# A GRU scan on one core: n's columns of W_hh copied by ScalarE as each chunk lands, band loads behind W_hh, and one round of Toeplitz products moved into step 7

## The chip, the cores and the metric

The kernel runs on one core of a Trainium2 chip. The metric is device time in microseconds (us), median of the runs; less is better.

## The reference, cut to what matters

```python
# x: (16, 256, 512) f32, cond: (16, 512); W_ih, W_hh: (512, 1536); b_ih, b_hh: (1536,)
x = x + causal_depthwise_conv(x, cond)   # 16 taps along T=256, one filter value per lag and channel
def cell(h, xt):
    gi = xt @ W_ih + b_ih                # split in three: i_r, i_z, i_n
    gh = h @ W_hh + b_hh                 # h_r, h_z, h_n
    r = sigmoid(i_r + h_r); z = sigmoid(i_z + h_z)
    n = tanh(i_n + r * h_n)
    h_new = (1 - z) * n + z * h
    return h_new, h_new
x = x + scan(cell, h0=cond, over=T)
```

Batch is 16, T is 256, the feature width F is 512, all float32.

## The kernel before

The scan is 256 steps, one after the other, t = 0 to 255. The features lie in C = 4 chunks of 128 partitions; the state and the gates are split in H = 2 halves f, of two chunks each. One step on TensorE is 32 matmuls h @ W_hh (`recur(t, f, c)`, L304, four matmuls of 192 columns each, one for each strip of 32 columns of the array). While VectorE, ScalarE and GpSimd turn the sums into the next h, TensorE fills the time with x @ W_ih for two steps ahead of need (`product(m, f, c)`, L294, four matmuls; a call for each chunk c, four calls a step). Each float32 matmul appears in the trace as two records, so a step's `recur` is 64 records and its products are 32. `pg` are the PSUM accumulators, `hp` the state, `s_h[f]` the semaphore that counts finished states of half f (1 at the start, t + 2 after step t).

**W_hh.** `whh` holds per chunk four blocks of F columns: n, r, z, n. The main loop reads the first three (n, r, z). SyncE loads r, z, n of each chunk into blocks 1 to 3 (L210, 768 KB a chunk, semaphore `s_whh[c]`), and then n of all chunks once more into block 0 (L211, 1024 KB, `s_whn`). Step 0 does not read block 0: `recur_first(f, c)` (L315, L318) takes r, z and the last block in two matmuls, 128 and 64 columns. Between its chunks stand matmuls on zeros, `IDLE` = 4 behind chunk 1 and 3 behind chunk 2 (L373), whose result nobody reads. Before step 1 TensorE waits for `s_whn`.

**The convolution.** Times 0 to 15 are done by VectorE and, for chunk 3, by TensorE. Times 16 to 47 come from TensorE: `turn(p, l, r)` (L332), for each half l of the features 16 rounds r of four matmuls of the band matrix `tz` with a window of x, `xw[l]`, into `pcv`. From time 48 on VectorE does it (L474). The dictionary `ROUNDS` says in which steps the rounds stand: half 0 in steps 6 and 7, half 1 in step 10. VectorE moves the result out of `pcv` (`spread`, steps 8 and 9 and step 11). The first round of a half waits for all eight of its `xw` transfers, and of half 0 also for the eight `tz` transfers.

**SyncE's queue.** After the W_hh transfers SyncE waits for all of them, `s_whn` too, and then goes through the steps: at step t it waits for `s_h[0]` >= t + 1, and issues what stands there: eight band transfers `tz` (L177) at t = 0 to 2 (2, 3 and 3), eight `xw[0]` transfers (L185) at t = 3 to 5 (2, 3, 3), eight `xw[1]` transfers at t = 6 to 8 (2, 3, 3), then later x windows `xb` (L198) and the output. Each `tz` and `xw` transfer is 128 KB in rows of 16 floats.

Of the kernel before, what the change touches and what calls it, by code (L numbers as in the profile page):

```python
# [7 lines left out]
ACT = mybir.ActivationFunctionType  # L8

P = 128  # L10
J, C, D = 4, 4, 32
B, T, F = 16, 256, 512
K = 16
# [16 lines left out]
FEW = 4  # L30
WARM = 6
LATE = 18
IDLE = {1: 4, 2: 3}
M2 = T // 2
RZ, IN, END = CH * D, 3 * CH * D, 4 * CH * D
Q = 3
# [3 lines left out]
def build(nc, x, cond, w_ih, w_hh, b_ih, b_hh, out):  # L40
    assert J * D == P
    ctx = ExitStack()
    with ctx:  # L43
# [20 lines left out]
        whh = sb("whh", [P, C, 4 * F])  # L64
# [82 lines left out]
        def share(total, steps, t):  # L147

            a, b = steps
            return range(total * min(max(t - a, 0), b - a) // (b - a), total * min(max(t + 1 - a, 0), b - a) // (b - a))  # L150


        ROUNDS = {(0, 0): (6, 8), (0, 1): (10, 11)}
        TURNED = {(0, 0): (8, 10), (0, 1): (11, 12)}
        SPANS = [(a - W2 - 4, a - 4) for a, _ in LONG]
        BAND = (0, 3)
# [12 lines left out]
        @block.sync  # L169
        def _(sp):  # L170
            def band(q):
                l, g = divmod(q, G)
                c, e = l * CH + g // 2, g % 2
                if q == 0:
                    sp.wait_ge(s_scr, 16)
                    sp.wait_ge(s_band, 1)
                sp.dma_start(tz[W2 * g:W2 * (g + 1), l, :, g * K:(g + 1) * K],  # L177
                             bass.AP(scratch, (e * C + c) * TAPS, [[1, W2], [2 * C * TAPS, P // 2], [1, K]])
                             ).then_inc(s_tz, 16)

            def load(p, l, q):
                i, g = divmod(q, G)
                t = W2 * p + TB * i
                c, e = l * CH + g // 2, g % 2
                sp.dma_start(xw[l][W2 * g:W2 * (g + 1), :, i, :],  # L185
                             x[:, c, t * B:(t + W2) * B].rearrange("(p e) (w b) -> e w p b", e=2, b=B)[e]
                             ).then_inc(s_xw[p][l], 16)

            def load_long(k, c, i):
                a, b = LONG[k]  # L190
                if i == c == k == 0:
                    sp.wait_ge(s_c3, 1)
                if i == 0 and k >= 2:
                    sp.wait_ge(s_long, len(EVERY) * (k - 2) + K * (c + 1))
                n = (K - 1 + b - a) * B
                at, to = n * i // PIECES, n * (i + 1) // PIECES
                first = (a - K + 1) * B
                sp.dma_start(window(k)[:, c, at:to], x[:, c, first + at:first + to]).then_inc(s_xb[k][c], 16)  # L198

            def store(k, c):  # L200
                a, b = STORES[k]
                sp.wait_ge(s_o, b)
                sp.dma_start(out[:, c, a * B:b * B], x1_of(c, a, b)).then_inc(s_out[k], 16)

            sp.dma_start(cnd[:, :, :], cond).then_inc(s_cnd, 16)  # L205
            sp.dma_start(xs[:, :, :], x[:, :, 0:TB * B]).then_inc(s_xs, 16)  # L206
            for c in range(C):
                sp.dma_start(wih[:, c, :, :], w_ih[:, c, :, :]).then_inc(s_wih[c], 16)  # L208
            for c in range(C):
                sp.dma_start(whh[:, c, F:], w_hh[:, c, :]).then_inc(s_whh[c], 16)  # L210
            sp.dma_start(whh[:, :, 0:F], w_hh[:, :, 2 * F:]).then_inc(s_whn, 16)  # L211
            for c in range(C):
                sp.wait_ge(s_whh[c], 16)
            sp.wait_ge(s_whn, 16)
            for t in range(T):
                sp.wait_ge(s_h[0], t + 1)
                for q in share(2 * G, BAND, t):
                    band(q)
                for (p, l), steps in WINDOWS.items():
                    for q in share(2 * G, steps, t):  # L220
                        load(p, l, q)
                for k in range(len(LONG)):
                    for c in range(C):
                        for i in share(PIECES, arriving(k, c), t):
                            load_long(k, c, i)
                for k, (a, b) in enumerate(STORES[:NB - 1]):
                    for c in share(C, (b, b + C), t):
                        store(k, c)
                for k, (a, b) in enumerate(STORES[NB - 1:-1], NB - 1):
                    if b == t:  # L230
                        sp.wait_ge(s_o, b)
                        sp.dma_start(out[:, :, a * B:b * B], x1_of(slice(None), a, b)).then_inc(s_out[k], 16)
            a, b = STORES[-1]
            sp.wait_ge(s_o, b)
            sp.dma_start(out[:, :, a * B:b * B], x1_of(slice(None), a, b)).then_inc(s_out[len(STORES) - 1], 16)
            for k in range(len(STORES)):
                sp.wait_ge(s_out[k], 16 * (C if k < NB - 1 else 1))
# [40 lines left out]
        def _(pe):  # L278
# [86 lines left out]
                pe.wait_ge(s_h[f], 1)  # L365
            for c in range(C):
                pe.wait_ge(s_whh[c], 16)
                for f in range(H):
                    i = recur_first(f, c)
                    if c == C - 1:  # L370
                        i.then_inc(s_gh[f], 1)
                for _ in range(IDLE.get(c, 0)):
                    pe.matmul(pcv[:, 0:512], zeros[:, 0:P], zeros[:, :], start=True, stop=True)  # L373
            for c in range(C):
                product(2, 0, c)
            pe.wait_ge(s_whn, 16)
            for t in range(1, T):
                m = t // 2
                if t % 2 == 0:
                    pe.wait_ge(s_tin[0], m + 1)  # L380
                    pe.wait_ge(s_tin[1], m + 1)
                pe.wait_ge(s_h[0], t + 1)
                recur(t, 0, 0)
                recur(t, 0, 1)
                recur(t, 1, 0)
                pe.wait_ge(s_h[1], t + 1)
                recur(t, 0, 2)
                recur(t, 0, 3).then_inc(s_gh[0], 1)
                recur(t, 1, 1)
                recur(t, 1, 2)  # L390
                recur(t, 1, 3).then_inc(s_gh[1], 1)
                if m + 2 < M2:
                    for c in range(C):
                        product(m + 2, t % 2, c)
                for (p, l), steps in ROUNDS.items():
                    for r in share(K, steps, t):
                        turn(p, l, r)

        @block.scalar
        def _(act):  # L400
            def seed(m, f):

                if m < Q:
                    act.wait_ge(s_bits, 2 * Q)
                    act.wait_ge(s_bc, H)
                else:
                    act.wait_ge(s_tn[f], 2 * (m - Q) + 2)
                act.activation(pg[m % Q][f][:, 0:END], bc[:, f, :], ACT.Copy).then_inc(s_seed[f], 1)  # L408

            act.dma_start(bih[:, :], b_ih).then_inc(s_small, 16)  # L410
            act.dma_start(bhh[:, :], b_hh).then_inc(s_small, 16)
            act.wait_ge(s_cp, 3)
            act.dma_start(scratch[:, :, :], cpad[:, :, :]).then_inc(s_scr, 16)
            act.wait_ge(s_eye, 2)
            act.wait_ge(s_cnd, 16)
            for lag in range(K):
                act.activation(diagonal(lag), eye[:, :], ACT.Copy, scale=cnd[:, C - 1, K - 1 - lag:K - lag]).then_inc(s_dg, 1)
            for m in range(Q):
                for f in range(H):
                    seed(m, f)  # L420
            act.wait_ge(s_c3, 1)
            act.activation(x1[:, C - 1, 0:TB * B], pcv[:, 0:TB * B], ACT.Copy).then_inc(s_ev, 1)
            act.activation(pre[:, :], cnd[:, 0, :], ACT.Sigmoid)
            act.wait_ge(s_zero, 4)
            for t in range(T):
                u = slice(t % 2 * B, (t % 2 + 1) * B)
                for f in range(H):
                    act.wait_ge(s_trz[f], t + 1)
                    act.activation(rz[:, f, :, :, 1].rearrange("p g (c b) -> p (g c) b", b=B), gt[:, f, :, u],  # L429
                                   ACT.Sigmoid).then_inc(s_rz[f], 1)  # L430
                    act.activation(zcp[:, f, ::2, :, 1], gt[:, f, CH:, u],  # L431
                                   ACT.Sigmoid, scale=-1.0).then_inc(s_zc[f], 1)
                    act.wait_ge(s_an[f], t + 1)
                    act.activation(nzh[:, f, ::2, :, 0], chunks(an[:, f, :, 1]), ACT.Tanh).then_inc(s_n[f], 1)  # L434
                if t % 2 and t // 2 + Q < M2:
                    for f in range(H):
                        seed(t // 2 + Q, f)
# [170 lines left out]
```

## Time and profile before

| | |
|---|---|
| median of 3 runs | 1035.78 us (1035.08 to 1035.82) |
| the profiled execution's own time | 1035.15 us |
| its span in the trace | 1033.4 us |
| mean granted TensorE clock, share of full | 0.996 |
| TensorE matmul busy | 1018.7 us, 99% |
| VectorE busy | 855.9 us, 83% |
| ScalarE busy | 396.8 us, 38% |
| GpSimd busy | 239.1 us, 23% |

Times in the rows are microseconds from the span's start unless marked ns. PE is TensorE, DVE VectorE, ACT ScalarE, POOL GpSimd, SP SyncE; SPq is its queue of issued transfers. The profiled execution took 1.75 us more than its span, for what lies around the span.

### The profile page before, as it was taken

How to read it: one execution, taken by the hardware profiler on the slowest of the kernel's cores; microseconds unless marked ns; L12 is line 12 of the kernel's file. 1: busy time of each engine (PE TensorE's matmuls, PEld its weight loads, DVE VectorE, ACT ScalarE, POOL GpSimd, SP SyncE). 2: the span in 40 equal slices, each digit the busy share in tenths (PEclk: the TensorE clock that was granted, in tenths of full speed). 3: DMA queues.
4: the chain of work that ended last, by engine and by line, in shares of the span. 5: the costliest groups of instructions: out<-in, count | busy, mean ns of one | idle time of the engine just before them, and what ended most of it. 6: DMA issues, size and time to landing. Idle time of an engine off the chain costs nothing.

```text
span 1033.4 us, 58398 instructions
## 1 busy us (share of the span) xinstructions
PE 1018.7 (99%) x24948; PEld 975.6 (94%) x24949; DVE 855.9 (83%) x2838; ACT 396.8 (38%) x1812; POOL 239.1 (23%) x782
## 2 busy tenths in 40 slices
PE   8899999999999999999999999999999999999997
PEld 6779999999999999999999999999999999999996
DVE  7548888888888888888888888888888887777554
ACT  4324334333333343433433433333333343343342
POOL 3212222222222222222222222222222222222222
PEclk9989999999999999999999999999999999999999
DMA  8851000010010101001010010100101000000000
GB/s 312 80 64 34 20 15 31 19 40 19 15 33 14 39 18 29 25 11 36 18 35 24 11 35 15 39 19 20 30 15 35 14 28 16 12 29 3 24 14 12
DMA packets 78930, 33.53 MB, mean 32 GB/s; under 512 B 56016, under 2 KB 77136, under 8 KB 78672
## 3 DMA queue, kind: packets, MB, share of 16 engines
q1 hardware_dynamic: 78240, 29.70, 11.5%
q8 instruction: 196, 3.21, 1.3%
q14 instruction: 62, 0.51, 0.2%
q10 hardware_dynamic: 432, 0.11, 0.0%
HBM read 21.31 MB, written 8.49 MB: 29 GB/s over the span
## 4 chain that ended last, share of the span: by engine, by line
PE 96%; DMA 2%; SPq 1%; DVE 0%; issue 0%; DVEq 0%; POOLq 0%; ACT 0%
PE pg L304 64%; PE pg L294 31%; DMA whh<-w_hh 2%; SPq L185 1%; PE pcv L332 0%; DMA xw<-x 0%; SPq L208 0%; SPq L210 0%; DVE hp L522 0%; DVE gn L501 0%; SPq L206 0%; SPq L205 0%; POOLq L43 0%; DVE an L509 0%; DVEq L520 0%
## 5 line engine op out<-in xcount | busy, mean ns | idle before, releaser
L304 PE MATMUL pg<-whh,hp 128*32 128x192 f32 x16320 | 718.6, 327 | 3.2 <-DVE hp L522 2.5
L304 PEld LDWEIGHTS pg<-whh,hp 128*32 128x32 f32 x16320 | 640.1, 110 | 28.5 <-DVE hp L522 2.3
L294 PE MATMUL pg<-wih,x 128*32 128x192 f32 x8192 | 386.4, 326 | 0.0
L270 POOL TENSOR_TENSOR nzh<-rz,hp 128x32 f32<-128x32 f32 x512 | 157.9, 308 | 788.2 <-ACT rz L429 788.2
L294 PEld LDWEIGHTS pg<-wih,x 128*32 128x32 f32 x8192 | 321.3, 110 | 11.6
L429 ACT ACTIVATE rz<-gt 128x64 f32<-128x64 f32 x512 | 135.9, 266 | 502.8 <-DVE gt L497 477.9
L474 DVE SCALAR_TENSOR_TENSOR x<-xb,cnd,x 128x512 f32<-128x512 f32 (+1 forms) x420 | 294.8, 702 | 7.9
L497 DVE STREAM_TRANSPOSE gt<-pg 128x128 f32<-128x128 f32 x512 | 160.1, 313 | 69.9 <-PE pg L304 61.8
L522 DVE TENSOR_TENSOR_SCAN hp<-zcp,nzh 128x96 f32<-128x96 f32 x512 | 173.3, 338 | 41.6 <-ACT nzh L434 41.0
L509 DVE TENSOR_TENSOR_SCAN an<-rz,gn 128x64 f32<-128x64 f32 x512 | 149.0, 291 | 51.8 <-ACT rz L429 51.6
L434 ACT ACTIVATE nzh<-an 128x32 f32<-128x32 f32 x512 | 120.7, 236 | 126.4 <-DVE an L509 126.4
L431 ACT ACTIVATE zcp<-gt 128x32 f32<-128x32 f32 x512 | 111.0, 217 | 0.0
L501 DVE STREAM_TRANSPOSE gn<-pg 128x64 f32<-128x64 f32 x512 | 107.0, 209 | 0.0
L408 ACT ACTIVATE pg<-bc 128x256 f32<-128x256 f32 x256 | 86.3, 369 | 0.0
L264 POOL TENSOR_TENSOR x<-x,hp 128x64 f32<-128x64 f32 x256 | 82.0, 320 | 0.7 <-DVE hp L522 0.7
L492 DVE STREAM_TRANSPOSE gn<-pg 128x64 f32<-128x64 f32 x256 | 58.0, 227 | 0.0
L474 DVE SCALAR_TENSOR_TENSOR x<-xb,cnd 128x512 f32<-128x512 f32 (+1 forms) x28 | 19.3, 690 | 0.1
L458 DVE SCALAR_TENSOR_TENSOR x<-xs,cnd,x 128x192 f32<-128x192 f32 (+11 forms) x45 | 11.6, 327 | 0.0
L332 PE MATMUL pcv<-tz,xw 128*32 128x64 f32 x256 | 5.0, 243 | 4.4 <-DMA xw<-x 4.4
L332 PEld LDWEIGHTS pcv<-tz,xw 128*32 128x32 f32 x256 | 4.6, 126 | 5.0 <-DMA xw<-x 4.8
L257 POOL MEMSET tz<- 128x8192 f32 x1 | 6.9, 6927 | 1.0 <-DVE bc L543 1.0
L340 PEld LDWEIGHTS pcv<-xs,xb 128*128 128x128 f32 x32 | 4.7, 196 | 0.3
(42 smaller groups left out, 47.1 us busy)
## 6 DMA issues: line engine op xcount, KB each, us to landing
xb<-x SPq DMA_DIRECT2D x96, 94.0 KB, 2.0
out<-x SPq DMA_DIRECT2D x60, 128.0 KB, 1.8
wih<-w_ih SPq DMA_DIRECT2D x4, 768.0 KB, 8.1
whh<-w_hh SPq DMA_DIRECT2D x4, 768.0 KB, 14.5
xw<-x SPq DMA_DIRECT2D x16, 128.0 KB, 4.5
whh<-w_hh SPq DMA_DIRECT2D x1, 1024.0 KB, 18.9
tz<-taps SPq DMA_DIRECT2D x8, 128.0 KB, 4.7
xb<-x SPq DMA_DIRECT2D x16, 62.0 KB, 1.9
```

What stands on the lines that cost most here:

```text
L270: pool.tensor_tensor(nzh[:, f, ::2, :, 1], chunks(rz[:, f, 1, :, 1]), h_of(t - 1, slice(f * CH, (f + 1) * CH)), ALU.mult).then_inc(s_zh[f], 1)
L294: i = pe.matmul(pg[m % Q][f][D * j:D * (j + 1), RZ:END], x1_of(c, 2 * m, 2 * m + 2), wih[:, c, :, :].rearrange("p (g k) (j d) -> p j g k d ...
L304: i = pe.matmul(pg[t // 2 % Q][f][D * j:D * (j + 1), 0:IN], hp[:, t % 2, 2 * c + 1 - t % 2:2 * c + 3 - t % 2, :, 1].rearrange("p u b -> p ...
L408: act.activation(pg[m % Q][f][:, 0:END], bc[:, f, :], ACT.Copy).then_inc(s_seed[f], 1)
L429: act.activation(rz[:, f, :, :, 1].rearrange("p g (c b) -> p (g c) b", b=B), gt[:, f, :, u], ACT.Sigmoid).then_inc(s_rz[f], 1)
L431: act.activation(zcp[:, f, ::2, :, 1], gt[:, f, CH:, u], ACT.Sigmoid, scale=-1.0).then_inc(s_zc[f], 1)
L434: act.activation(nzh[:, f, ::2, :, 0], chunks(an[:, f, :, 1]), ACT.Tanh).then_inc(s_n[f], 1)
L474: dve.scalar_tensor_tensor(o, xx[:, c, (K - 1 - lag) * B:(K - 1 - lag + n) * B], cnd[:, c, K - 1 - lag:K - lag], o if lag else now, ALU.mu ...
L497: dve.transpose(gt[:, f, :, :].rearrange("p c r -> p (c r)"), pg[t // 2 % Q][f][:, RZ:IN]).then_inc(s_trz[f], 1)
L501: dve.transpose(gn[:, t // 2 % 2, :, f, :, :, 0].rearrange("p u c b -> p c u b"), pg[t // 2 % Q][f][:, 0:RZ]).then_inc(s_tn[f], 1)
L509: dve.tensor_tensor_scan(an[:, f].rearrange("p n s -> p (n s)"), rz[:, f, 0].rearrange("p n s -> p (n s)"), gn[:, t // 2 % 2, t % 2, f].re ...
L522: dve.tensor_tensor_scan(hp[:, (t + 1) % 2, a:a + n].rearrange("p c b s -> p (c b s)"), zcp[:, f, 0:n].rearrange("p c b s -> p (c b s)"), ...
```

## The change

Five edits. The extra load of n's columns is gone; ScalarE copies block 3 of `whh` to block 0 as each chunk lands, and counts `s_whn` up by one for each. Step 0 uses the ordinary `recur` for chunks 0 to 2, behind the wait for that copy, and `recur_first` for chunk 3 alone. SyncE no longer waits for `s_whn` before the band transfers. One matmul on zeros behind chunk 2 is dropped. All 16 rounds of half 0 stand in step 7, and rounds that share a step with products stand between the product calls, four behind each.

```diff
-IDLE = {1: 4, 2: 3}
+IDLE = {1: 4, 2: 2}
...
-        ROUNDS = {(0, 0): (6, 8), (0, 1): (10, 11)}
+        ROUNDS = {(0, 0): (7, 8), (0, 1): (10, 11)}
...
             for c in range(C):
                 sp.dma_start(whh[:, c, F:], w_hh[:, c, :]).then_inc(s_whh[c], 16)
-            sp.dma_start(whh[:, :, 0:F], w_hh[:, :, 2 * F:]).then_inc(s_whn, 16)
             for c in range(C):
                 sp.wait_ge(s_whh[c], 16)
-            sp.wait_ge(s_whn, 16)
...
             for c in range(C):
                 pe.wait_ge(s_whh[c], 16)
+                if c < C - 1:
+                    pe.wait_ge(s_whn, c + 1)
                 for f in range(H):
-                    i = recur_first(f, c)
-                    if c == C - 1:
-                        i.then_inc(s_gh[f], 1)
+                    if c < C - 1:
+                        recur(0, f, c)
+                    else:
+                        recur_first(f, c).then_inc(s_gh[f], 1)
...
-            pe.wait_ge(s_whn, 16)
+            pe.wait_ge(s_whn, C)
...
-                if m + 2 < M2:
-                    for c in range(C):
+                for c in range(C):
+                    if m + 2 < M2:
                         product(m + 2, t % 2, c)
-                for (p, l), steps in ROUNDS.items():
-                    for r in share(K, steps, t):
-                        turn(p, l, r)
+                    for (p, l), steps in ROUNDS.items():
+                        for r in share(K, steps, t):
+                            if r * C // K == c:
+                                turn(p, l, r)
...
             act.activation(pre[:, :], cnd[:, 0, :], ACT.Sigmoid)
+            for c in range(C):
+                act.wait_ge(s_whh[c], 16)
+                act.activation(whh[:, c, 0:F], whh[:, c, 3 * F:], ACT.Copy).then_inc(s_whn, 1)
```

TensorE's instructions at steps 6 and 7 in the kernel before, with their waits. A row is one or more matmuls of a line; L304 is `recur`, L294 `product`, L332 `turn`.

```order
L294 MATMUL pg<-wih,x 32x192 [waits s_first,s_seed0]
L294 MATMUL pg<-wih,x 32x192 x15
L332 MATMUL pcv<-tz,xw 32x64 [waits s_tz,s_xw00]
L332 MATMUL pcv<-tz,xw 32x64 x31
L304 MATMUL pg<-whh,hp 32x192 [waits s_h0]
L304 MATMUL pg<-whh,hp 32x192 x11
L304 MATMUL pg<-whh,hp 32x192 [waits s_h1]
L304 MATMUL pg<-whh,hp 32x192 x19
L294 MATMUL pg<-wih,x 32x192 [waits s_first,s_seed1]
L294 MATMUL pg<-wih,x 32x192 x15
L332 MATMUL pcv<-tz,xw 32x64 x32
```

The same engine from step 7's `recur` to its end in the changed kernel (L302, L292 and L330 are the same three functions there).

```order
L302 MATMUL pg<-whh,hp 32x192 [waits s_h0]
L302 MATMUL pg<-whh,hp 32x192 x11
L302 MATMUL pg<-whh,hp 32x192 [waits s_h1]
L302 MATMUL pg<-whh,hp 32x192 x19
L292 MATMUL pg<-wih,x 32x192 [waits s_first,s_seed1]
L292 MATMUL pg<-wih,x 32x192 x3
L330 MATMUL pcv<-tz,xw 32x64 [waits s_tz,s_xw00]
L330 MATMUL pcv<-tz,xw 32x64 x15
L292 MATMUL pg<-wih,x 32x192 x4
L330 MATMUL pcv<-tz,xw 32x64 x16
L292 MATMUL pg<-wih,x 32x192 x4
L330 MATMUL pcv<-tz,xw 32x64 x16
```

The wait for `tz` and `xw[0]` stood behind step 6's products and ahead of step 7; it now stands behind step 7's `recur` and a quarter of its products.

ScalarE between its last work on the first 16 times and step 0 in the changed kernel: the four rows of L428 are new, the rest is as before.

```order
L424 ACTIVATE x<-pcv 128x256 [waits s_c3]
L425 ACT_TABLE_LOAD
L425 ACTIVATE pre<-cnd 128x16
L428 ACTIVATE whh<-whh 128x512 [waits s_whh0]
L428 ACTIVATE whh<-whh 128x512 [waits s_whh1]
L428 ACTIVATE whh<-whh 128x512 [waits s_whh2]
L428 ACTIVATE whh<-whh 128x512 [waits s_whh3]
L434 ACTIVATE rz<-gt 128x64 [waits s_trz0,s_zero]
```

ScalarE's first gate of step 0 (L434) stands behind the fourth copy now.

SyncE's queue around the W_hh transfers, before (-) and now (+).

```order
 L208 DMA wih<-w_ih 128x1536 x4
 L210 DMA whh<-w_hh 128x1536 x4
-L211 DMA whh<-w_hh 128x4x512
-L177 DMA tz<-taps 32x64x16 [waits s_whn,s_h0,s_whh3,s_scr,s_whh2,s_band,s_whh1,s_whh0]
+L177 DMA tz<-taps 32x64x16 [waits s_h0,s_whh3,s_scr,s_whh2,s_band,s_whh1,s_whh0]
 L177 DMA tz<-taps 32x64x16
```

One transfer and one wait are gone ahead of the first band transfer.

## Rows read from the trace of the kernel before

**Rows 1.** The page's part 1: busy time of each engine, share, instructions.

```profile
PE 1018.7 (99%) x24948; PEld 975.6 (94%) x24949; DVE 855.9 (83%) x2838; ACT 396.8 (38%) x1812; POOL 239.1 (23%) x782
```

**Rows 2.** TensorE's waits, whole span: us in total, times, longest.

```profile
PE pcv L332 <- DMA xw<-x: 4.4, 1, 4.4
PE pg L304 <- DVE hp L522: 2.5, 3, 0.9
```

**Rows 3.** TensorE's timeline, 0 to 100 us: start, length, instructions, idle before.

```profile
18.65 0.45 PE L315 MATMUL pg<-whh,hp 128*32 128x128 f32 x8 [0.23 <-DMA whh<-w_hh]
...
20.53 0.45 PE L315 MATMUL pg<-whh,hp 128*32 128x128 f32 x8
...
21.37 0.82 PE L373 MATMUL pcv<-zeros 128*128 128x512 bf16 x3
22.46 0.45 PE L315 MATMUL pg<-whh,hp 128*32 128x128 f32 x8 [0.27 <-DMA whh<-w_hh]
...
23.18 1.50 PE L294 MATMUL pg<-wih,x 128*32 128x192 f32 x31
25.40 2.81 PE L304 MATMUL pg<-whh,hp 128*32 128x192 f32 x64 [0.72 <-DMA whh<-w_hh]
...
47.52 1.48 PE L294 MATMUL pg<-wih,x 128*32 128x192 f32 x32
53.44 1.94 PE L332 MATMUL pcv<-tz,xw 128*32 128x64 f32 x64 [4.43 <-DMA xw<-x]
55.15 4.38 PE L304 MATMUL pg<-whh,hp 128*32 128x192 f32 x64
59.36 1.47 PE L294 MATMUL pg<-wih,x 128*32 128x192 f32 x32
60.66 1.07 PE L332 MATMUL pcv<-tz,xw 128*32 128x64 f32 x64
61.55 2.77 PE L304 MATMUL pg<-whh,hp 128*32 128x192 f32 x64
64.15 1.47 PE L294 MATMUL pg<-wih,x 128*32 128x192 f32 x32
...
73.25 1.96 PE L332 MATMUL pcv<-tz,xw 128*32 128x64 f32 x128
75.04 2.82 PE L304 MATMUL pg<-whh,hp 128*32 128x192 f32 x64
```

**Rows 4.** Stretches: length, busy (records) per engine, PEclk, DMA share, GB/s.

```profile
25.40:49.00 23.60, 23.60 (x576) 18.77 (x576) 12.92 (x54) 9.12 (x42) 5.39 (x18) 1.00 0.83 78
49.01:53.44 4.43, 0.00 (x0) 0.00 (x0) 0.36 (x1) 0.00 (x0) 0.00 (x0) 0.79 0.97 90
53.44:55.15 1.71, 1.71 (x64) 1.71 (x68) 0.00 (x0) 0.00 (x0) 0.00 (x0) 0.50 0.86 80
55.15:59.36 4.21, 4.21 (x77) 2.73 (x69) 0.52 (x3) 0.38 (x2) 0.03 (x1) 0.61 0.92 87
```

**Rows 5.** SyncE's queue, timeline of single issues: start, length.

```profile
25.63 0.33 SPq L177 DMA_DIRECT2D tz<-taps  x1
...
26.02 1.90 SPq L177 DMA_DIRECT2D tz<-taps  x1
```

**Rows 6.** The chain that ended last, near 49 us: start, length, what.

```profile
49.16 4.24 DMA xw<-x
```

**Rows 7.** VectorE's timeline: the states' scans of step 0 (both halves) and step 4.

```profile
24.42 0.36 DVE L522 TENSOR_TENSOR_SCAN hp<-zcp,nzh 128x96 f32<-128x96 f32 x1
...
25.26 0.36 DVE L522 TENSOR_TENSOR_SCAN hp<-zcp,nzh 128x96 f32<-128x96 f32 x1
...
40.35 0.31 DVE L522 TENSOR_TENSOR_SCAN hp<-zcp,nzh 128x96 f32<-128x96 f32 x1
```

**Rows 8.** ScalarE's timeline, 0 to 60 us, around its idle time.

```profile
11.81 0.38 ACT L422 ACTIVATE x<-pcv 128x256 f32<-128x256 f32 x1 [0.28 <-PE pcv L340]
...
23.53 0.26 ACT L429 ACTIVATE rz<-gt 128x64 f32<-128x64 f32 x1 [9.81 <-DVE gt L497]
```

## The prediction

> **What bounds the kernel now.** I first read the busy shares: TensorE's matmul row is busy 99% of the span, the next engine 83% [rows 1]. So the kernel is a string of TensorE work, and a change can only pay where TensorE waits, runs at a lower clock, or does work that could go. Next I read its waits: in the whole span one is long, 4.4 us in front of `turn` for a transfer of `xw`; the rest are under 1 us each, 2.5 us of them in three waits for the state [rows 2]. The timeline then gives the regular step: `recur` takes 2.60 us (61.55 to 64.15), a step's products 1.30 us (59.36 to 60.66), together 3.90 us, and eight rounds of `turn` 0.89 us, sixteen 1.79 us [rows 3]. A call of `recur` or `product` is an eighth or a quarter of that, 0.325 us.
>
> Two places stand out. Step 1 starts at 25.40, 0.72 us after TensorE's last work, for the second load of n [rows 3]. And step 6's products, started at 47.52, are issued by 48.82, but the first round starts at 53.44 [rows 3]: 4.62 us from issue to issue, 4.43 of it idle. The stretches show what follows: in the idle one the granted clock averages 0.79, in the rounds behind it 0.50, which is the lower level of 1.2 GHz, in step 7's `recur` 0.61 [rows 4]. These eight rounds took 1.71 us where the next eight took 0.89, and this `recur` 4.21 us (55.15 to 59.36) where others take 2.60 [rows 3]. So the stall costs 4.62 + 0.82 + 1.61 = 7.05 us.
>
> What is late is SyncE's queue of short-row transfers. The 1st starts at 25.63, right behind the landing of n, the 2nd at 26.02 [rows 5]; the 16th, the last of half 0, at 49.16, and it lands 4.24 us later, at 53.40 [rows 6]. That is 14 intervals of 1.65 us from 2nd to 16th. At h waits it hardly stops: `s_h[0]` for t = 5 is counted at 40.66 [rows 7], and the queue was by then only at its 11th transfer (26.02 + 9 x 1.65 = 40.9). The DMA engines' share is 0.83 to 0.97 all along, at 78 to 91 GB/s [rows 4]; I take the stream to run at the pace of its short rows.
>
> **The change, part by part.**
>
> *The load of n goes (1024 KB).* The last chunk of W_hh lands by 22.46, where TensorE starts on it [rows 3]; it was ahead in the queue, so I leave it there. Step 1 then needs the state and TensorE. h of half 0 is scanned at 24.42 + 0.36 = 24.78 and half 1 at 25.62 [rows 7]; the products before it are issued by 23.18 + 1.30 = 24.48 [rows 3]. With 0.05 us from semaphore to matmul, step 1 starts at 24.83. Half 1's state is first needed three calls later, 25.81, after 25.62. Gain: 25.40 - 24.83 = **0.57 us**. What is late next there is the state, not a load.
>
> *Four copies of 128x512 on ScalarE.* The trace has none. No table load is added (ScalarE's listing). The nearest is a 128x256 copy at 0.38 us; with 128x64 at 0.26 [rows 8] the slope gives 0.54 us. Bounds: 0.38 (no slower than half the width) and 0.76 (twice it). ScalarE is idle for 9.81 us ahead of 23.53 [rows 8], so the copies need nobody's time; the fourth ends at 22.46 + 0.54 = 23.0, at most 23.22, ahead of 23.53, where the first gate starts. What waits behind them is that gate, so the cover is 0.3 us even at the upper bound.
>
> *Step 0 waits for copies.* Chunk 1: copied from 18.65, `recur` at about 19.25 in place of 18.65; two calls of 0.325 and four fillers of 0.27 (0.82 for three [rows 3]) give 20.98. Chunk 2 had landed by 20.53, where TensorE took it up, so its copy is through by 21.13; two calls, 21.78, two fillers, 22.32. Chunk 3, whose n is read from its own block, starts at 22.46 as before. With 0.76 us a copy it is 22.54, a loss of 0.08. `recur` in place of `recur_first` streams the same columns. So: **0**, hidden behind the landing of chunk 3.
>
> *Band loads earlier.* First issue 25.63 came 0.23 us behind step 1's release at 25.40; now 22.46 + 0.23 = 22.69, so the stream starts 2.94 us earlier. Its first gate is the third transfer's, `s_h[0]` at 24.78; two issues take until 23.08 + 1.90 = 24.98, so it does not hold. The stream keeps its pace and the last of half 0 lands at 53.40 - 2.94 = 50.46.
>
> *Rounds of half 0 in step 7.* Step 6's eight rounds leave; step 7 starts at 24.83 + 6 x 3.90 = 48.23, its `recur` ends at 50.83, the first quarter of products at 51.16. The first round needs 50.46: **0.7 us to spare**, no wait. Then come the other products, 0.98, and 16 rounds, 1.79: step 8 starts at 53.93. Before it started at 61.55 [rows 3]. The difference, **7.62 us**, is 7.05 + 0.57.
>
> The clock deserves weighing. The row says: after 4.43 us without a matmul the level was 1.2 GHz; the three 0.8 to 0.9 us waits for a state near the end [rows 2] are idle too, and the mean clock of the span is 0.996 (the table above). The sum therefore takes full clock throughout, and the 0.82 + 1.61 us as won with the wait. The Trainium skill, "TensorE: Matmul & The Clock Gate", section "HAM oscillation — how this bites in real kernels", says that waits between bursts of matmuls send the array to half rate, so that the next burst starts slow. By that rule, the trace agrees at 53 us, and the change also does something against it: it makes TensorE wait in step 0 and drops a filler, which is the third case below.
>
> *Second half.* The 24th transfer starts 8 x 1.65 after the 16th (49.16 - 2.94 + 13.2 = 59.4) and lands near 63.7. States gate t = 7 and 8 no later: step 4 started at 25.40 + 3 x 3.90 = 37.10 and had its state 3.56 us later (40.66 [rows 7]), so step 7 has it at 51.8. Step 10 starts at 53.93 + 7.80 = 61.73, its first round stands at 64.66: 1 us to spare. Steps 11 on see the same order as before, where nobody waited.
>
> Sum: the profiled execution's 1035.15 less 7.62 gives 1027.5 us. It lies 0.63 below the median of three; from the median it is 1028.2. I say **1028.1**.
>
> **The rivals.**
>
> *A: as summed*, 1027.0 to 1028.8, chance 0.71.
>
> *B: a round still waits a little.* The margins, 0.7 us in step 7 and 1 us in step 10, hang on a pace that I assume. Single issues vary from 0.33 to 1.90 us [rows 5]; for it speaks that the engines are near their limit. If half 0 landed where it did, at 53.44, the wait would be 53.44 - 51.16 = 2.28 us: 1030.4. Against it: the queue's head truly moves 2.9 us. Chance 0.13, 1028.8 to 1030.6.
>
> *C: the clock drops in step 0.* From the end of chunk 0 (18.65 - 0.23 = 18.42 [rows 3]) to 22.46 TensorE now idles about 0.83 + 0.15 + 0.14 us where it idled about 0.7, with a filler less. The price is what the rows at the lower level cost, 1.61 for a step's `recur`, 2.43 with what surrounds it: 1029.8 to 1030.6. Against it: no gap exceeds 0.9 us, and three such near the end did no visible harm. Chance 0.10.
>
> *D: slower than before.* The stream of 24 transfers is now asked to run beside a TensorE that never pauses. With interval p the 24th lands at 23.08 + 22p + 4.24, and step 11 starts 2.77 us later (0.98 + 1.79). It started at 75.04 [rows 3]; equality is at p = 2.04 us. At p = 2.2 it is 78.5, 3.5 us late: 1039.3 us. For it: a share of 0.97 leaves no reserve [rows 4]. Against it: from 25.40 to 49.00 the same stream ran at 1.65 beside a busy TensorE. Chance 0.02.
>
> *E: the gain is given back elsewhere* (between these), within 0.2%: 0.04. Nothing in the rows speaks for it.
>
> **How the numbers follow.** The likeliest is A. A range of 1027.0 to 1030.6 holds A, B and most of C, about 0.9 by these chances; I keep the upper end since B and C each end there. About 0.2%, 2 us, is what a measurement of this kernel can tell from no change. A, B and C are all faster by over that: 0.94; D and part of E slower: 0.02; the rest same: 0.04.
>
> **What the profile would show.** Step 1 near 24.8, released by a VectorE scan and not by W_hh; four ScalarE copies of 0.4 to 0.8 us, the last over by 23.3; chunk 3 of step 0 at 22.46; first `tz` issue near 22.7; no wait for `xw`; four `turn` groups in step 7 beside products, each at full clock; step 8 near 53.9; step 11 near 67.4 instead of 75.04. The prediction is wrong if a round waits for `xw`, if the granted clock leaves 1.00 between 18 and 64 us, or if later steps lose the 3.90 us rhythm.

## The result, and the profile after

The changed kernel takes 1029.58 us (median of 4 runs, 1029.06 to 1031.5) against 1035.43 (4 runs, 1034.81 to 1035.82) beside it: ratio 0.9947, 95% interval 0.993 to 0.9965. That is 5.85 us less. Two later sets of runs gave 1030.09 and 1029.87, ratios 0.9945 (0.9933 to 0.9958) and 0.995 (0.9938 to 0.9963). The forecast was 1028.1; direction, size and range held, and 1.5 us of the gain did not come. The median lies above case A (1027.0 to 1028.8, chance 0.71). The range held it because it also took in the times of B and C, and B did not happen. The profiled execution took 1029.06 us, span 1027.3. (The title speaks of one round moved into step 7; the diff moves the eight rounds of step 6 there.)

TensorE's waits in the changed kernel, whole span (line: us in total, times, longest):

```profile
PE pg L302 <- DVE hp L527: 2.7, 4, 0.9
PE pg L302 <- ACT whh L428: 2.4, 2, 1.6
...
PE pg L302 <- issue: 0.5, 1, 0.5
```

The 4.4 us wait for `xw` [rows 2] is gone. Two new lines stand there: waits for the copies in step 0, and one stop of 0.5 us that no semaphore explains ("issue").

TensorE's timeline of the changed kernel, for the pieces of [rows 3]:

```profile
18.00 0.86 PE L302 MATMUL pg<-whh,hp 128*32 128x192 f32 x16 [1.55 <-ACT whh L428]
19.73 0.86 PE L302 MATMUL pg<-whh,hp 128*32 128x192 f32 x16 [0.87 <-ACT whh L428]
20.52 1.04 PE L374 MATMUL pcv<-zeros 128*128 128x512 bf16 x4
21.63 0.86 PE L302 MATMUL pg<-whh,hp 128*32 128x192 f32 x16
22.42 0.61 PE L374 MATMUL pcv<-zeros 128*128 128x512 bf16 x2
22.96 0.45 PE L313 MATMUL pg<-whh,hp 128*32 128x128 f32 x8
...
25.41 2.81 PE L302 MATMUL pg<-whh,hp 128*32 128x192 f32 x64 [0.25 <-DVE hp L527]
...
48.81 2.81 PE L302 MATMUL pg<-whh,hp 128*32 128x192 f32 x64
51.41 0.54 PE L292 MATMUL pg<-wih,x 128*32 128x192 f32 x8
51.74 0.66 PE L330 MATMUL pcv<-tz,xw 128*32 128x64 f32 x32
...
54.50 0.85 PE L302 MATMUL pg<-whh,hp 128*32 128x192 f32 x13
55.81 2.31 PE L302 MATMUL pg<-whh,hp 128*32 128x192 f32 x50 [0.46 <-issue]
```

The reader is to see three things. Step 7 is as forecast: its `recur` starts at 48.81, the first round at 51.74 without a wait, and 54.50 - 48.81 = 5.69 us is 2.60 + 1.30 + 1.79 to the hundredth. Step 1 starts at 25.41 and not at 24.83: nothing was won at the head, for chunk 3 of step 0 (L313) starts at 22.96 in place of 22.46. And step 8 stops behind its 13th record. A `recur` of 64 records takes 2.60 us, 0.0406 us a record: 13 x 0.0406 us after 54.50 is 55.03, it goes on at 55.81, so 0.78 us are lost.

ScalarE's copies in the changed kernel, and two of SyncE's issues, the first `tz` and the last `xw[0]`:

```profile
17.22 0.63 ACT L428 ACTIVATE whh<-whh 128x512 f32<-128x512 f32 x1 [3.79 <-DMA whh<-w_hh]
18.96 0.63 ACT L428 ACTIVATE whh<-whh 128x512 f32<-128x512 f32 x1 [1.10 <-DMA whh<-w_hh]
20.85 0.63 ACT L428 ACTIVATE whh<-whh 128x512 f32<-128x512 f32 x1 [1.26 <-DMA whh<-w_hh]
22.67 0.63 ACT L428 ACTIVATE whh<-whh 128x512 f32<-128x512 f32 x1 [1.19 <-DMA whh<-w_hh]
```

```profile
22.86 0.33 SPq L177 DMA_DIRECT2D tz<-taps  x1
...
45.75 1.23 SPq L185 DMA_DIRECT2D xw<-x  x1
```

The stream of short-row transfers starts 2.77 us earlier than in [rows 5], and its 16th issue 3.41 us earlier than in [rows 6]. That 16th transfer lands 4.82 us after its start, at 50.57 (forecast 50.46), which is 1.2 us ahead of the first round at 51.74. Each copy waits for its chunk; the chunks land 0.2 to 0.3 us later than in the profile of before. That is within what executions differ by: over the 13 profiles of this document the last chunk lands between 21.97 and 22.76, and the latest is that of experiment one, whose W_hh loads are those of before.

### The profile page after: what moved, and what is told of

Read it like the earlier page. It is cut to its first block, busy times and chain, and to the rows that moved or that the text cites. A ratio compares the mean times of both kernels' runs of the same rounds, so it can differ in the third digit from the quotient of the medians.

```text
span 1027.3 us, 58306 instructions
## 1 busy us (share of the span) xinstructions
PE 1015.4 (99%) x24900; PEld 991.9 (97%) x24900; DVE 857.2 (83%) x2838; ACT 401.0 (39%) x1816; POOL 240.8 (23%) x782
## 4 chain that ended last, share of the span: by engine, by line
PE 97%; issue 1%; POOL 1%; DVE 0%; DMA 0%; POOLq 0%; DVEq 0%; ACT 0%
PE pg L302 65%; PE pg L292 32%; POOL tz L255 1%; PE pcv L330 0%; DMA cnd<-cond 0%; DVE hp L527 0%; DVE gn L506 0%; POOLq L43 0%; POOL nzh L268 0%; POOL nzh L253 0%; DVE an L514 0%; POOL cpad L246 0%; POOL rz L251 0%; POOL zcp L252 0%; DVE gt L502 0%
## 5 line engine op out<-in xcount | busy, mean ns | idle before, releaser
L302 PE MATMUL pg<-whh,hp 128*32 128x192 f32 x16368 | 727.3, 326 | 5.7 <-DVE hp L527 2.7
L302 PEld LDWEIGHTS pg<-whh,hp 128*32 128x32 f32 x16368 | 658.6, 110 | 18.5 <-issue 3.2
L292 PE MATMUL pg<-wih,x 128*32 128x192 f32 x8192 | 395.6, 326 | 0.0
L292 PEld LDWEIGHTS pg<-wih,x 128*32 128x32 f32 x8192 | 332.9, 110 | 5.8
L434 ACT ACTIVATE rz<-gt 128x64 f32<-128x64 f32 x512 | 136.4, 266 | 485.3 <-DVE gt L502 461.7
L506 DVE STREAM_TRANSPOSE gn<-pg 128x64 f32<-128x64 f32 x512 | 110.0, 215 | 0.0
L497 DVE STREAM_TRANSPOSE gn<-pg 128x64 f32<-128x64 f32 x256 | 59.1, 231 | 0.0
L330 PE MATMUL pcv<-tz,xw 128*32 128x64 f32 x256 | 5.8, 219 | 0.0
L330 PEld LDWEIGHTS pcv<-tz,xw 128*32 128x32 f32 x256 | 5.7, 110 | 0.1
L428 ACT ACTIVATE whh<-whh 128x512 f32<-128x512 f32 x4 | 2.5, 631 | 7.3 <-DMA whh<-w_hh 7.3
```

The costliest lines, as they stand in the source:

```text
L292: i = pe.matmul(pg[m % Q][f][D * j:D * (j + 1), RZ:END], x1_of(c, 2 * m, 2 * m + 2), wih[:, c, :, :].rearrange("p (g k) (j d) -> p j g k d ...
L302: i = pe.matmul(pg[t // 2 % Q][f][D * j:D * (j + 1), 0:IN], hp[:, t % 2, 2 * c + 1 - t % 2:2 * c + 3 - t % 2, :, 1].rearrange("p u b -> p ...
L506: dve.transpose(gn[:, t // 2 % 2, :, f, :, :, 0].rearrange("p u c b -> p c u b"), pg[t // 2 % Q][f][:, 0:RZ]).then_inc(s_tn[f], 1)
```

## The experiments

**One: the rounds moved, nothing else.**

```diff
 # the kernel before, with
-        ROUNDS = {(0, 0): (6, 8), (0, 1): (10, 11)}
+        ROUNDS = {(0, 0): (7, 8), (0, 1): (10, 11)}
 # and turn() between the product calls, as in the change
```

> The kernel before with only the move of half 0's rounds into step 7, between the products; n is still loaded a second time and the band loads still wait for it. By the sum's terms: step 7 starts at 48.82, its first quarter of products ends at 51.75, and the last xw[0] transfer lands at 53.4, so one wait of 1.7 us is left where 4.4 us were; step 8 starts near 56.2 in place of 61.55: 5.3 us faster than before, if the clock stays at full through a wait of 1.7 us. Theory 1 (the move of the rounds carries most of the gain, the earlier loads only the rest): ratio near 0.9949. Theory 2 (the earlier loads carry it, as the wait was for a transfer): a ratio near 0.998, with a wait of over 3 us left and the granted clock below 1.00 behind it.

Measured: 1030.69 (1029.34 to 1031.14) against 1035.34, ratio 0.9952 (0.994 to 0.9964): 4.65 us less. Its profile, timeline of TensorE in step 7:

```profile
52.64 0.65 PE L332 MATMUL pcv<-tz,xw 128*32 128x64 f32 x32 [0.56 <-DMA xw<-x]
53.11 0.51 PE L294 MATMUL pg<-wih,x 128*32 128x192 f32 x8
```

A wait of 0.56 us is left, and the first quarter of rounds behind it takes 0.47 us, as at full clock (0.44 in the changed kernel's profile); the granted clock from 48 to 56 us is 1.00. Theory 1 holds; from issue to issue the wait was 0.90 us and not 1.7 in this execution, the shortest of the five (1029.34), as the last transfer landed at 52.6.

**Two: the copies and the earlier loads, without the move.**

```diff
 # the changed kernel, with
-        ROUNDS = {(0, 0): (7, 8), (0, 1): (10, 11)}
+        ROUNDS = {(0, 0): (6, 8), (0, 1): (10, 11)}
 # and turn() behind all product calls again
```

> The changed kernel with the rounds put back: eight in step 6 and eight in step 7, both behind all products. The second load of n is gone, ScalarE copies, the band loads start 2.8 us earlier. Theory 1: a wait of about 1.7 us for xw is left in front of the rounds of step 6 (landing near 50.6, products issued by 48.8), the clock stays at full, so 4.4 + 2.4 us shrink to 1.7 us: about 5.3 us faster than before. Theory 2: the lower clock follows any wait of this kind; then only the 2.8 us of the landing are gained, ratio near 0.9973. In both step 1 starts near 25.4 as in the changed kernel, since step 0 still waits for the copies.

Measured: 1031.09 (1030.28 to 1031.86), ratio 0.9958 (0.9945 to 0.9972): 4.25 us less. TensorE's timeline:

```profile
19.41 1.50 PE L302 MATMUL pg<-whh,hp 128*32 128x192 f32 x16 [1.06 <-ACT whh L427]
...
24.02 0.45 PE L313 MATMUL pg<-whh,hp 128*32 128x128 f32 x8
...
26.48 2.81 PE L302 MATMUL pg<-whh,hp 128*32 128x192 f32 x64 [0.25 <-DVE hp L526]
...
51.32 1.10 PE L330 MATMUL pcv<-tz,xw 128*32 128x64 f32 x64 [1.23 <-DMA xw<-x]
52.24 2.79 PE L302 MATMUL pg<-whh,hp 128*32 128x192 f32 x64
```

The wait in front of the rounds is 1.23 us and the clock stays full behind it (eight rounds in 0.92 us, `recur` in 2.60): theory 1, with a granted clock of 1.00 from 48 to 64 us. Its statement on the head was wrong: step 1 starts at 26.48. Chunk 1's 16 records take 1.50 us where they take 0.86 elsewhere. The clock had fallen in step 0: it was 0.50 from 19.5 to 21 us. Four of this experiment's five runs have the mean clock of 0.998 that goes with it, and that is part of why 4.25 us came where 5.3 were expected.

One and two together tell where the gain is: alone they give 4.65 and 4.25 us, both together (four, beside them on the same chip) 5.25. They overlap, since either one shortens the wait enough to keep the clock up behind it.

**Three: step 0 as before the change.**

```diff
 # the changed kernel, with
-IDLE = {1: 4, 2: 2}
+IDLE = {1: 4, 2: 3}
...
                 pe.wait_ge(s_whh[c], 16)
-                if c < C - 1:
-                    pe.wait_ge(s_whn, c + 1)
                 for f in range(H):
-                    if c < C - 1:
-                        recur(0, f, c)
-                    else:
-                        recur_first(f, c).then_inc(s_gh[f], 1)
+                    i = recur_first(f, c)
+                    if c == C - 1:
+                        i.then_inc(s_gh[f], 1)
```

> The changed kernel with step 0 as in the kernel before: recur_first for all chunks, four and three fillers, no wait for a copy before step 1. Theory 1 (the copies of 0.63 us and the order copy, recur, filler pushed chunk 3 of step 0 from 22.46 to 22.96): chunk 3 starts within 0.1 us of its landing, step 1 starts near 24.9, and the kernel is 0.5 us faster than the changed one. Theory 2 (the transfers of W_hh themselves landed later in the changed kernel's profiled run): step 1 starts near 25.2 to 25.4 here too, less than 0.2 us gained. The 0.8 us stop of TensorE in step 8 with no releaser is expected to stay in both, as nothing here touches it.

**Four: the changed kernel beside them.**

> The changed kernel once more, on the same chip as the others, for the spread of its times (1029.06 to 1031.5 in four runs, where the kernel before spread over 1.0 us). Theory 1: an unsteady piece of up to 2 us, a wait for xw or a stop of TensorE near step 8, differs from run to run; the times spread over more than 1.5 us again. Theory 2: the 1031.5 was a single outlier, the rest lies within 1 us of 1029.3.

Measured: three takes 1028.78 (1028.1 to 1028.85), ratio 0.9933 (0.992 to 0.9945); four takes 1030.09 (1028.76 to 1030.56), a spread of 1.8 us. Five runs of each; 1.3 us between the medians, though the intervals overlap. First three's timeline, then four's:

```profile
22.64 0.45 PE L313 MATMUL pg<-whh,hp 128*32 128x128 f32 x8 [0.18 <-DMA whh<-w_hh]
...
25.10 2.81 PE L302 MATMUL pg<-whh,hp 128*32 128x192 f32 x64 [0.25 <-DVE hp L524]
```

```profile
19.63 1.51 PE L302 MATMUL pg<-whh,hp 128*32 128x192 f32 x16 [0.86 <-ACT whh L428]
21.48 1.28 PE L374 MATMUL pcv<-zeros 128*128 128x512 bf16 x3 [0.33 <-ACT whh L428]
22.69 0.86 PE L302 MATMUL pg<-whh,hp 128*32 128x192 f32 x16
23.48 0.61 PE L374 MATMUL pcv<-zeros 128*128 128x512 bf16 x2
24.02 0.45 PE L313 MATMUL pg<-whh,hp 128*32 128x128 f32 x8
```

And four's stretches (length, busy per engine, PEclk, DMA share, GB/s):

```profile
17.92:19.57 1.65, 0.85 (x16) 0.47 (x16) 1.65 (x10) 0.63 (x1) 0.00 (x0) 0.83 1.03 432
19.57:21.00 1.43, 1.37 (x16) 0.68 (x16) 1.15 (x8) 0.23 (x1) 0.00 (x0) 0.50 0.61 255
21.00:23.50 2.50, 2.17 (x24) 0.88 (x22) 0.00 (x0) 1.03 (x2) 0.00 (x0) 0.72 0.06 16
```

In three, chunk 3 starts with its landing, and step 1 at 25.10, 0.31 us ahead of the changed kernel's profile. Times of two executions mix the chain with the chance of the landing: eight, the changed kernel again, starts step 1 at 25.08, as its last chunk landed at 22.35. So the chain is read inside each execution, from the last landing (which starts the fourth copy) to chunk 3's first matmul. That is 0.29 us in the changed kernel's profile, 0.23 to 0.27 in six, eight, nine and eleven, 0.50 in seven, and 0.02 in three and ten, which have no chain. So theory 1 has the mechanism right, and the chain costs about 0.3 us. Four shows a second piece: the clock at 0.50 of full, 1.2 GHz, in step 0, chunk 3 at 24.02 instead of 22.96, 1.06 us later. Measured from the last landing, chunk 3 starts 1.45 us behind it in four, and 1.67 and 1.65 in two and five, whose profiles show the same fall. Three also had no stop in step 8, which neither theory expected.

**Five: the transfers of half 1 left out.**

```diff
-                        load(p, l, q)
+                        if l == 0:
+                            load(p, l, q)
 # turn() of half 1 waits for and reads xw[0]
```

> The changed kernel with the eight xw[1] transfers left out; half 1's rounds read xw[0] instead (so times 16 to 47 of the second half of the features are computed from the wrong window). Theory 1: the stop of TensorE behind the 13th record of step 8 (0.5 and 0.7 us idle with no releaser in two profiles of the changed kernel) is its program waiting to be fetched while the DMA engines carry xw[1]; without these transfers the engines are idle at that time and the stop goes: step 8 to step 9 is 3.90 us, and the kernel gains 0.8 to 1.0 us. Theory 2: the stop belongs to that place in the program whatever the DMA engines do; it stays at 0.5 to 0.7 us and the time is that of the changed kernel within 0.3 us.

**Six: three fillers behind chunk 0.** `IDLE = {0: 3, 1: 4, 2: 2}`.

> The changed kernel with three matmuls on zeros more, behind chunk 0 of step 0, in the 0.9 us in which it waits for the second copy. Theory 1 (the granted clock falls to its lower level in step 0 in some runs, because TensorE is idle there while it waits for copies, and costs about 1 us in them): the clock is 1.00 from 17 to 25 us, the chunks start where they did in the changed kernel's first profile, chunk 3 near 22.9, no run shows a mean clock under 0.999, and the median falls by 0.3 to 0.8 us against the changed kernel. Theory 2 (the fall has to do with the 1.1 to 1.6 us idle ahead of chunk 0): the lower clock is still there in some runs, mean clock 0.997 or 0.998, spread as before.

**Seven: the rounds behind the products**, both halves, all else as changed.

> The changed kernel with the 16 rounds of step 7 in one block behind the products, and half 1's in step 10 too. Theory 1 (only the step counts, for the transfers land before the first quarter of products ends): same time as the changed kernel within 0.3 us. Theory 2 (the place between products hides part of a round, or saves a wait for the state): slower by over 0.5 us.

**Eight: the changed kernel beside them.**

> The changed kernel beside the three others on this chip. Median 1029.3 to 1030.1 as twice before; runs with a mean clock of 0.997 or 0.998 are the longer ones by about 1 us, and the profiled execution has a stop of 0.4 to 0.8 us behind the 13th record of step 8.

Measured, against 1035.72: five 1029.67 (1028.3 to 1030.38), six 1029.38 (1028.84 to 1030.24), seven 1029.22 (1028.53 to 1029.41), eight 1029.87 (1029.21 to 1031.52); ratios 0.9944, 0.9943, 0.9941, 0.995, their intervals all overlap. Timeline of TensorE at the stop, five, six, seven and eight in turn:

```profile
55.18 0.85 PE L303 MATMUL pg<-whh,hp 128*32 128x192 f32 x13
56.22 2.31 PE L303 MATMUL pg<-whh,hp 128*32 128x192 f32 x50 [0.19 <-issue]
```

```profile
54.27 0.81 PE L302 MATMUL pg<-whh,hp 128*32 128x192 f32 x10
55.46 2.31 PE L302 MATMUL pg<-whh,hp 128*32 128x192 f32 x51 [0.37 <-issue]
```

```profile
52.85 2.00 PE L330 MATMUL pcv<-tz,xw 128*32 128x64 f32 x128
54.64 0.85 PE L302 MATMUL pg<-whh,hp 128*32 128x192 f32 x13
55.95 2.31 PE L302 MATMUL pg<-whh,hp 128*32 128x192 f32 x50 [0.46 <-issue]
```

```profile
54.16 0.85 PE L302 MATMUL pg<-whh,hp 128*32 128x192 f32 x13
55.75 2.31 PE L302 MATMUL pg<-whh,hp 128*32 128x192 f32 x50 [0.74 <-issue]
```

Three fillers more ahead of it, and the stop comes three records sooner, 10 for 13: it belongs to a place of TensorE's program and not to a semaphore. Without the transfers of half 1 it is 0.19 us where it is 0.37 to 0.74 with them: smaller in this one profile, but there, so theory 1 of five did not hold. Seven shows that the place of the rounds between the products is worth nothing measurable: the transfers have landed before the first quarter of products ends. For the clock, each run lists its mean: eight's runs at 0.998 and 0.997 took 1031.52 and 1031.01, its other three 1029.21 to 1029.87. Six and seven had no run below 0.999; in seven, whose step 0 is that of the changed kernel, five runs are too few to say more than chance. Six's median is 0.49 us below eight's, as its theory 1 asked, but the intervals overlap. Five's 1029.67 against eight's 1029.87 says nothing on the stop, since three of five's runs had the lower clock.

**Nine: the rounds split over steps 7 and 8.** `ROUNDS = {(0, 0): (7, 9), ...}` in the changed kernel.

> The changed kernel with half 0's 16 rounds split over steps 7 and 8, eight in each, two behind each quarter of the products. Theory 1 (TensorE's stop in step 8 is its program arriving late behind a burst of short matmuls: it has come at one place of the program, behind record 13, or record 10 with three fillers more ahead, in all five profiles with this step 7): half the burst is spread over 3.9 us more, the stop goes or falls under 0.2 us, and step 7 to step 9 is 3.9 x 2 + 1.79 = 9.6 us; 0.5 to 1.0 us faster than the changed kernel. Theory 2 (the stop belongs to the place in the program): it stays at 0.4 to 0.7 us idle, the time is unchanged. In both, step 0's lower clock still turns up in some runs.

**Ten: the same on three's kernel.**

> The kernel of the third experiment (step 0 as before the change) with the split as well. It had neither the lower clock in step 0 nor the stop. Theory 1: nothing is left to win, 1028.8 within 0.4 us, no run with a mean clock under 0.999. Theory 2 (unseen short stops near step 8 make its 0.7 us of spread): 0.5 us faster, spread under 0.5 us.

**Eleven: six once more.**

> The kernel with three fillers behind chunk 0 once more, to count runs. With the changed kernel's step 0, 12 of 29 runs had a mean clock of 0.997 or 0.998; with the fillers 0 of 5. Theory 1 (idle TensorE in step 0 drops the clock, the fillers prevent it): again no run under 0.999. Theory 2 (chance): one to three of five are at 0.998 or lower and 1 us or more longer than the rest.

Measured, against 1035.61: nine 1029.11 (1028.62 to 1030.1), ratio 0.9938 (0.9925 to 0.995); ten 1028.23 (1027.64 to 1028.68), ratio 0.9927 (0.9915 to 0.994), the lowest median of all; eleven 1029.58 (1029.44 to 1029.81), ratio 0.9941 (0.9928 to 0.9955). Nine's timeline, then ten's:

```profile
53.57 2.81 PE L302 MATMUL pg<-whh,hp 128*32 128x192 f32 x64
56.17 1.19 PE L292 MATMUL pg<-wih,x 128*32 128x192 f32 x24
```

```profile
57.60 0.65 PE L330 MATMUL pcv<-tz,xw 128*32 128x64 f32 x29
58.62 0.25 PE L330 MATMUL pcv<-tz,xw 128*32 128x64 f32 x2 [0.38 <-issue]
```

In nine the stop of step 8 is gone: 64 records in one piece, 2.60 us to the products. A smaller one stands in its step 10: at 68.14, 0.36 us lie between two records of the rounds, 0.14 of them idle. In ten, which as three had shown none, one of 0.38 us came, among step 8's rounds. So the split moves or removes a stop according to where the program stands, and is no cure. Ten's ratio is 0.0006 below three's, 0.6 us, and the intervals overlap: neither of its theories is decided. The lower clock: nine has two runs of five with it (0.998 and 0.997, 1029.68 and 1030.1; the others 1028.62 to 1029.11). Eleven had none.

## Why the prediction was right, and where 1.5 us went

**Right: the wait and what follows it.** The term of 7.05 us (wait, slow rounds, slow `recur`) came in full: step 7 to step 8 is 5.69 us in the profile, by the parts of the sum. The stream of transfers moved with its head as said: 2.77 us at the head, 2.83 at the last landing of half 0. Of the 1.2 us to spare in step 7, 0.58 came from the late head; without it the 0.7 of the sum would have been 0.6. What the sum did not say is that it holds two remedies, either of which alone brings over 4 us.

**Wrong: "0, hidden behind the landing of chunk 3", and with it the 0.57 us of the head.** The sum had `recur` of chunk 2 at 21.13, done at 21.78, fillers to 22.32, ahead of 22.46. Measured: the third copy starts at 20.85 (20.53 taken), lasts 0.63 us (0.54 taken, inside the bounds), `recur` starts at 21.63, 0.15 us behind its end, the fillers only 0.79 us later (0.65 taken: turning from `recur` to a filler costs 0.14), and chunk 3 at 22.96. Since its chunk had landed by 22.67, 0.3 us of that is the chain of copy, `recur` and fillers, and 0.2 the later landing. Experiment three, which takes the chain away, starts chunk 3 with its landing. What bounds step 1 is the state, as forecast (0.25 us [<- DVE hp]), but 0.58 us later. The last 0.09 us of these is the sum's 0.05 from semaphore to matmul. Before step 1 that fitted a landed transfer; here half 0's state is ready at 25.27 and the matmul starts at 25.41, 0.14 us behind it, and 0.15 in three.

**Wrong: "full clock throughout".** Rival C had 0.10, and it counted TensorE's idle time only from the end of chunk 0. The longest idle stretch lies ahead of chunk 0, whose `recur` waits for a copy too: 1.55 us in the profile after, where it was 0.40 before. With the changed kernel's step 0 (changed kernel three times, two, five, seven, nine) 14 of 34 runs had a mean clock of 0.998 or 0.997. In the changed kernel itself those five took 1030.32 to 1031.52, the other nine 1028.76 to 1030.09: 1.8 us between the two medians. That this lies within the priced 1.6 to 2.4 is partly luck: by the traces of two, four and five the fall costs 1.2 to 1.4 us (1.45 to 1.67 us from landing to chunk 3, less 0.3), and the rest of the 1.8 was not located. In those three profiles the fall stands in step 0; for the runs without a profile only the mean is known. With three fillers behind chunk 0 none of 10 runs fell, and with step 0 as before none of 15 (one, three and ten). If neither edit mattered, none in those 25 against 14 in 34 would be a chance of about 1 in 10,000, and the ten with fillers alone 1 in 80. That idle in step 0 is what lets it fall is therefore shown as far as counts can; what decides in which run is open: nine's profile has 1.71 and 0.87 us idle and full clock, four's 1.65 and 0.86 and the lower one. The Trainium skill, "TensorE: Matmul & The Clock Gate", section "HAM oscillation — how this bites in real kernels", says that waits between bursts of matmuls send the array to half rate. The trace agrees in kind: in the three profiles with the fall no single wait in step 0 was over 1.65 us, and it was enough there.

**Missed: the stop in step 8**, 0.78 us in the profile after and 1.06 in eight's (0.74 idle). No rival had it. D asked whether the stream bears a TensorE that never pauses; here TensorE stops, and it does so without half 1's stream too. All seven profiles with 16 rounds in step 7 and the changed or filled step 0 have the stop (after, four to eight, eleven), at the same place of the program: behind TensorE's 1104th or 1105th matmul record, counted from the start. Ten's stands behind the 1234th. A third place, behind the 1485th or 1486th, falls into step 10's rounds, where in two, five, eight, nine and eleven 0.2 to 0.6 us pass between two records. The traces also show the program itself arriving, as DMA packets of the kind "instruction". The page of the profile after (queue, kind: packets, MB, share):

```profile
q8 instruction: 196, 3.21, 1.3%
```

These are packets of 16 KB, one for every 254 of TensorE's 49,800 records of matmuls and weight loads; by that count they are TensorE's, though no view names the engine. Every one of these 13 stops ends 1.2 to 1.7 us behind the end of such a packet: in the profile after the packet ran from 53.13 to 54.50, TensorE reached the place at 55.03, and it went on at 55.81. In one and three it reached the same place 1.28 and 1.21 us behind the packet's end (54.99 against 53.71, 53.57 against 52.36), and there was next to nothing to wait for; in two, nine, ten and the kernel before it was later still. So the stop is the next part of the program arriving late, as theory 1 of nine had it: with the short records, step 7 uses up 224 matmul records in 5.69 us, where a plain step uses 96 in 3.90. The other half of theory 1 of five fails: with no xw[1] transfers beside it the packet took 1.30 us, where it took 0.96 to 1.38 with them. What starts a packet, and what passes between its end and the first matmul behind it, is open.

The profiled executions differ by 6.09 us: 7.62 less 0.58 for the head, less 0.78 for the stop, is 6.26; the last 0.17 us were lost in later steps and not located.

## What to carry to other kernels

Price a wait together with the clock behind it: 4.6 us of wait cost 7.05, and two different edits that each only shorten it each won back over 4 us, so such gains do not add. Where short instructions stand in a dense block, look at the instruction packets of the trace: a stop without a semaphore may be the program arriving late, and where it falls depends on the count of instructions ahead. Before putting a copy into a start-up chain that is paced by landings, add up wait, copy, use and filler for each link, with 0.1 to 0.2 us for each change of engine or of matmul form; where the first reader can take the original (three), leave the copy off its path. And look at the spread of runs and each run's mean clock, not only at the median: it is what set 5 of 14 runs, 1.8 us longer at the median, apart from the rest.

## What the hardware showed that was not expected

A 128x512 float32 copy on ScalarE takes 0.63 us in every one of its records. Behind the 128 short `turn` records of step 7 (one block of 1.79 us in seven, between products elsewhere) TensorE stopped for 0.19 to 0.74 us idle, with no semaphore, at one place of its program, 1.2 to 1.7 us behind the end of an instruction packet. And after a wait of 1.23 us the next matmuls ran at full clock (two), while in another place 0.86 us behind 1.65 came with the lower level (four).
